# Cross attention of a decoder: scores seven pairs ahead, keys three batches ahead, queries stacked for two batches

## The chip, the cores and the metric

One core of a Trainium2 chip runs the whole kernel in one launch. The metric is the device time of that launch in microseconds. Three runs of the kernel before took 4714.99, 4725.56 and 4725.31 us; their median is 4725.31.

## The reference

A decoder of four layers works on x, 32 batches of 56 tokens of 128 features, all in float32. Layers 1, 2 and 3 each have a cross attention to the same context of 1500 rows for each batch, and that is the part that the change touches:

```python
Q = (query @ Wq + bq).reshape(B, Sq, H, D).transpose(0, 2, 1, 3)   # query = layernorm(x): 32 x 56 x 128
K = (key @ Wk + bk).reshape(B, Sk, H, D).transpose(0, 2, 1, 3)     # key = value = ctx: 32 x 1500 x 128
V = (value @ Wv + bv).reshape(B, Sk, H, D).transpose(0, 2, 1, 3)
scores = jnp.einsum('bhqd,bhkd->bhqk', Q, K) / jnp.sqrt(jnp.float32(D))   # H = 16 heads, D = 8
attn = jax.nn.softmax(scores, axis=-1)
out = jnp.einsum('bhqk,bhkd->bhqd', attn, V).transpose(0, 2, 1, 3).reshape(B, Sq, E)
x = x + (out @ Wo + bo)
```

Layer 2 divides by the root of 128 instead. The other parts (self attention, a recurrence, mixtures of experts, a linear and a rotary attention) stay as they are.

## The kernel before

`decoder` (L2597) runs one stage after the other; `cross_attention` (L893) is called for layers 1, 2 and 3. Each engine has its own program in it, with the order of its work written out by hand, and semaphores between the engines.

The sixteen heads are eight pairs. A score product keeps float32 precision with bfloat16 matmuls: keys and queries are each split into three bfloat16 parts (high, middle, low), and six products of parts are wanted. So 96 rows are stacked, six slots (`SLOTS`) of 16 features, by DMAs on SP's queue (L984 for keys, L989 for queries): six DMAs for each half (four pairs) of a batch. Source buffers (`key_parts`) and stacked buffers (`keys`, `queries`) are double, the context `ctx_t` is threefold, and three banks hold one pair's scores.

The main loop has a pass i for each batch, and a pass has eight steps, one for each pair. In step p of pass i TensorE (L1122) does, in this order:

- `scores_by_key(i, p)` (L1063, matmuls L1072): twelve matmuls that give the scores with keys on the partitions, less the row maximum, which sits as additional rows of the stacked queries. It waits for the exponential of the pair before, since the three TURNED banks are single;
- in steps 3 and 7 `turn_tops` (L1058, L1061), which transposes the row maxima of four pairs; it waits for GpSimd's `split_tops` (L1230, operations L1234 to L1238);
- in steps 1 to 3 a third of the keys of batch i + 2, `make_keys` (L1026, L1034); in step 4 `fold` (L1089, L1098) of batch i - 1; in steps 5 to 7 a third of the values of batch i + 1, `make_values` (L1036, L1045). All of these share one bank, TURNS;
- `scores` (L1048, L1055) for the pair LEAD = 6 steps ahead: three matmuls of 500 keys, each of which waits until VectorE has taken the maximum of the pair before out of its bank;
- in steps 0 and 4 `mix_values` (L1076, L1085): 96 matmuls of probabilities by values for four pairs.

ScalarE (L1207) has `exponentials` (L1182, L1184) in each step, `place_others` (L1178, L1180) ahead of it in steps 0 and 4, `keep_mixed` (L1187) in steps 1 and 5, and behind the exponential the copy of a third of the keys (`keep_keys` L1165, L1171) or values (`keep_values` L1173, L1175) out of TURNS. VectorE (L1368) has `place_first` (L1339, L1341) in steps 3 and 7, the three row maxima of a pair in each step (`row_tops` L1323, L1326), `join_tops` (L1328) behind the last pair of a half, `keep_mix` (L1343) in step 4, and behind that `last_parts` (L1311, L1315 to L1321), which splits the last third of the keys of batch i + 2. GpSimd (L1261) splits the other two thirds (`high_part` L1247, L1250 and L1252; `low_parts` L1254, L1257 and L1259) and does `split_tops` between them. SP (L1010) loads context i + 3, then stacks both halves of batch i + 2 (`stack`, L973).

Ahead of the loop a head makes the normalisation, the queries and the keys of batch 0 (`lead_keys` L1021, `lead_high_part` L1289, `lead_low_parts` L1240, L1243), and the loop starts at pass -1, in which only the parts that run ahead have work.

## Time and profile before

| | |
|---|---|
| median of three runs | 4725.31 us |
| the profiled execution: its own time | 4729.11 us |
| the profiled execution: its span | 4727.3 us |
| mean granted TensorE clock | 0.921 of full |
| instructions | 107462 |

The span is that of the one profiled execution, from its first to its last record; its own time is measured around it and is 1.8 us longer. Engine names in rows: PE is TensorE's matmuls and PEld its weight loads, DVE is VectorE, ACT is ScalarE, POOL is GpSimd, SPq is SP's DMA queue. A timeline row is start, busy time, engine, line of the kernel, output and input, count, and in brackets the idle time of the engine ahead of it with what ended it. A row with a count merges neighbours; ends of matmuls are modelled and can overlap the next start.

### The profile page before, as it was taken

Reading aid. Unit: us, or ns where it says so; the run is one execution under the profiler, and the core shown is the slowest. Engines: PE = TensorE matmul, PEld = TensorE weight load, DVE = VectorE, ACT = ScalarE, POOL = GpSimd, SP = SyncE. Lnnn points to the kernel's source line nnn. Section 1 sums busy time; section 2 is a strip of 40 time slices with the busy share of each in tenths; the row PEclk is TensorE's granted clock in tenths of the full one; section 3 lists DMA queues with packets and bytes.
Section 4 is the critical chain, followed back from the end, with each engine's and each line's share of the span. In section 5 each row is a group of like instructions: output and inputs, shape, how many; then the busy total and the mean of one; then the engine's idle time right before and its main releaser. Section 6 shows DMA issues by size and latency. Waiting matters only on the chain. (4 is left out here: it accounts for less than half of the span.)

```text
span 4727.3 us, 107462 instructions
## 1 busy us (share of the span) xinstructions
PE 3885.6 (82%) x44766; PEld 2680.4 (57%) x44766; DVE 2978.1 (63%) x4986; ACT 2181.7 (46%) x2885; POOL 1144.9 (24%) x1441
## 2 busy tenths in 40 slices
PE   7987559999996977799999979866779999995498
PEld 5864226666664446466666654333346666663376
DVE  5632468877774445488777743355668787773643
ACT  2234436656663233266666643433346666663010
POOL 0000024444440000144444410021434444430000
PEclk9989869999997999899999989978789999996689
DMA  3035035555551410355555511000045555550366
GB/s 131 0 117 201 2 88 134 139 133 137 136 135 33 115 45 0 68 140 134 139 138 138 135 44 63 24 4 4 0 108 141 134 140 137 137 129 1 81 178 159
DMA packets 251804, 463.48 MB, mean 98 GB/s; under 512 B 135598, under 2 KB 143278, under 8 KB 251086
## 3 DMA queue, kind: packets, MB, share of 16 engines
q1 hardware_dynamic: 251406, 457.76, 38.1%
q8 instruction: 301, 4.93, 0.4%
q14 instruction: 97, 0.79, 0.0%
HBM read 212.85 MB, written 1.72 MB: 45 GB/s over the span
## 5 line engine op out<-in xcount | busy, mean ns | idle before, releaser
L1326 DVE TENSOR_REDUCE x_bank_top<-ps 112x1 f32<-112x500 f32 x2304 | 1409.7, 670 | 457.9 <-PE ps L1055 446.2
L1184 ACT ACTIVATE x_probs_t<-ps 128x1344 f32<-128x1344 f32 x768 | 990.9, 1290 | 309.1 <-PE ps L1072 296.3
L1055 PE MATMUL ps<-x_keys,x_queries 96*112 96x500 bf16 x2304 | 697.2, 387 | 62.8 <-DVE x_bank_top L1326 34.7
L1072 PEld LDWEIGHTS ps<-x_queries,x_keys 128*128 128x128 bf16 x9216 | 504.1, 98 | 189.6 <-ACT x_probs_t L1184 90.6
L1072 PE MATMUL ps<-x_queries,x_keys 128*128 128x112 bf16 x9216 | 585.8, 213 | 30.9 <-ACT x_probs_t L1184 25.0
L1055 PEld LDWEIGHTS ps<-x_keys,x_queries 96*112 96x112 bf16 x2304 | 288.7, 131 | 391.9 <-DVE x_bank_top L1326 198.2
L1085 PE MATMUL ps<-x_probs_t,x_values 128*32 128x112 f32 x18432 | 491.2, 263 | 4.1 <-ACT x_probs_t L1184 4.1
L1085 PEld LDWEIGHTS ps<-x_probs_t,x_values 128*32 128x32 f32 x18432 | 444.4, 111 | 51.0 <-issue 43.0
L1250 POOL TENSOR_TENSOR x_key_part<-x_key_whole,x_nothing 128x500 bf16<-128x500 f32 x186 | 231.3, 1244 | 826.0 <-ACT x_key_whole L1171 826.0
L1034 PE MATMUL ps<-x_ctx_t,x_wk 128*128 128x500 f32 x558 | 311.3, 640 | 25.5 <-ACT x_key_whole L1171 15.5
L1045 PE MATMUL ps<-x_wv,x_ctx_t 128*128 128x128 f32 (+1 forms) x2304 | 328.8, 286 | 1.7 <-issue 1.6
L1274 POOL MEMSET x_nothing<- 128x500 f32 x3 | 1.5, 514 | 1180.6 <-issue 1180.6
L1045 PEld LDWEIGHTS ps<-x_wv,x_ctx_t 128*128 128x128 f32 (+1 forms) x2304 | 280.3, 191 | 8.4 <-issue 1.8
L1189 ACT COPY x_mixed<-ps 128x112 f32<-128x112 f32 x192 | 48.4, 252 | 480.3 <-PE ps L1085 480.3
L1171 ACT ACTIVATE x_key_whole<-ps,x_bk 128x500 f32<-128x500 f32 x279 | 188.3, 675 | 127.0 <-PE ps L1034 103.6
L1257 POOL TENSOR_TENSOR x_key_part<-x_key_left,x_nothing 128x500 bf16<-128x500 f32 x186 | 233.7, 1256 | 7.5
L1517 PE MATMUL ps<-xn_lead,e_w 128*128 128x448 f32 x512 | 224.9, 546 | 4.2 <-DMA e_share<-m_weight_rows 4.2
L1259 POOL TENSOR_TENSOR x_key_part<-x_key_left,x_key_part 128x500 bf16<-128x500 f32 x186 | 218.0, 1172 | 14.6
L1544 ACT ACTIVATE e_silu<-ps 128x448 f32<-128x448 f32 x192 | 104.3, 543 | 249.5 <-PE ps L1517 249.5
L1252 POOL TENSOR_TENSOR x_key_left<-x_key_whole,x_key_part 128x500 f32<-128x500 f32 x186 | 211.6, 1138 | 14.6
L1523 PE MATMUL ps<-e_hidden,e_w 128*128 128x448 f32 x384 | 181.5, 554 | 9.1 <-DVE e_hidden L1562 5.0
L1175 ACT COPY x_values<-ps 128x512 f32<-128x512 f32 x288 | 168.2, 584 | 38.6 <-PE ps L1045 28.7
(478 smaller groups left out, 5340.2 us busy)
## 6 DMA issues: line engine op xcount, KB each, us to landing
x_keys<-x_key_part SPq DMA_DIRECT2D x1152, 192.0 KB, 3.5
x_ctx_t<-in_ctx_t SPq DMA_DIRECT2D x96, 750.0 KB, 4.6
cm_ctx_n<-in_ctx_n SPq DMA_DIRECT2D x32, 768.0 KB, 6.0
cm_ctx_t<-in_ctx_t SPq DMA_DIRECT2D x32, 750.0 KB, 8.3
x_queries<-x_query_part SPq DMA_DIRECT2D x1152, 14.0 KB, 2.3
e_share<-m_weight_scratch SPq DMA_DIRECT2D x32, 490.0 KB
e_spread_out<-m_slot_scratch SPq DMA_DIRECT2D x32, 490.0 KB
e_share<-m_weight_rows SPq DMA_DIRECT2D x32, 448.0 KB, 5.8
```

The costliest lines, as they stand in the source:

```text
L1034: nc.tensor.matmul(ps[:, TURNS, 0:KB], wk[:], ctx_t[i % CONTEXTS][:, KB * n:KB * n + KB], start=True, stop=True).then_inc(k_done, 1)
L1045: mm = nc.tensor.matmul(ps[0:ROWS[k], TURNS, P * c:P * c + P], ctx_t[i % CONTEXTS][:, CHUNK[k]], wv[:], start=True, stop=True)
L1055: nc.tensor.matmul(ps[0:RW, n, 0:KB], queries[i % 2][0:TALL, p, :], keys[i % 2][0:TALL, p, KB * n:KB * n + KB], start=True, stop=True).the ...
L1072: mm = nc.tensor.matmul(ps[:, TURNED + c // VC, RW * (c % VC):RW * (c % VC) + RW], keys[i % 2][:, p, KT * c:KT * c + KT], queries[i % 2][: ...
L1085: mm = nc.tensor.matmul(ps[32 * g:32 * g + 32, MIX, RW * h:RW * h + RW], values[i % 2][0:ROWS[c], c, (PF + 1) * p:(PF + 1) * p + 32], prob ...
L1184: nc.scalar.activation(probs_t[PROBS[p]].rearrange("k (n c) r -> k n (c r)", c=VC), ps[:, TURNED:TURNED + VR, 0:VC * RW], ACT.Exp, scale=s ...
L1250: nc.gpsimd.tensor_tensor(part[0][:, cols], key_whole[n][:], nothing[:], ALU.add).then_inc(k_high, 1)
L1252: nc.gpsimd.tensor_tensor(key_left[0][:], key_whole[n][:], part[0][:, cols], ALU.subtract).then_inc(k_rest, 1)
L1257: nc.gpsimd.tensor_tensor(part[1][:, cols], key_left[0][:], nothing[:], ALU.add).then_inc(k_mid, 1)
L1259: nc.gpsimd.tensor_tensor(part[2][:, cols], key_left[0][:], part[1][:, cols], ALU.subtract).then_inc(k_low, 1)
L1326: nc.vector.tensor_reduce(bank_top[0:RW, p, n:n + 1], ps[0:RW, n, 0:KB], AX_X, ALU.max).then_inc(topped, 1)
L1517: mm = nc.tensor.matmul(ps[:, 4 + 2 * (n % 2) + m, 0:CT], w[u][:, s, m, :], tokens[c], start=True, stop=True)
```

## The change

- **Lead.** LEAD goes from 6 to 7, so scores run seven pairs ahead; `turn_tops` and `place_first` move from steps 3 and 7 to steps 2 and 6.
- **Keys.** `make_keys` and `keep_keys` work on batch i + 3 instead of i + 2 and move from steps 1 to 3 to steps 5 to 7, on TensorE behind the step's scores; values move from steps 5 to 7 to steps 1 to 3. The loop starts at pass -2.
- **High parts.** For the second and last third ScalarE writes the bfloat16 high part straight from the bank, with an activation of its own ahead of the copy. GpSimd makes the high part of the first third and the middle and low parts of all three (`key_third`); `last_parts` on VectorE is gone. GpSimd's order in a pass is the split of the first half of batch i + 1, two thirds, the split of the second half, the last third.
- **Stacking.** Keys and queries have semaphores of their own. Queries are stacked for two batches at once, so six query DMAs of twice the bytes serve a half of two batches; ScalarE's queue issues the first six. SP's pass has the two halves of the keys with queries and the context between them, and contexts are loaded four batches ahead.
- **Head.** GpSimd fills the value buffers with ones ahead of `lead_low_parts`, not behind it.
- Waits follow: `make_keys` and `make_values` wait for `mix_kept` and `added` of other batches, `fold` and `project` for the work that now comes before them on the shared bank.

The core of the diff (buffers' indices that follow from the new shape of `queries`, removed functions and declarations are left out):

```diff
-LEAD = 6
+LEAD = 7
...
-    KEY_STEPS, VALUE_STEPS, FOLD_STEP = (1, 2, 3), (5, 6, 7), 4
-    BY_POOL = NB_ - 1
    TURNED, MIX, TURNS = 3, 6, 7
+    VALUE_STEPS, FOLD_STEP, KEY_STEPS = (1, 2, 3), 4, (5, 6, 7)
...
-        queries = [sbuf("queries%d" % u, [P, PR, RW], BF16) for u in range(2)]
+        queries = [sbuf("queries%d" % u, [P, PR, 2, RW], BF16) for u in range(2)]
...
+        def query_slots(engine, e, h, s):
+            source = slice(64 * h, 64 * h + 64)
+            queries_of = query_parts[QUERY_PART[s]][source]
+            engine.dma_start(queries[e % 2][s:TALL:SLOTS, HP_ * h:HP_ * h + HP_].rearrange("r p b n -> r (p b n)"),
+                             queries_of[:, 2 * e:2 * e + 2].rearrange("f b c s -> f (b c s)")).then_inc(queries_stacked[e % 2][h], 16)
...
@@ sync @@
+            def stack_keys(i, h):
+                u = i % 2
+                wait(sp, turned_done, PR * (i - 2) + HP_ * (h + 1))
+                if i == 0:
+                    sp.wait_ge(lead_low, NB_)
+                else:
+                    sp.wait_ge(k_low, NB_ * i)
+                source = slice(64 * h, 64 * h + 64)
+                for s in range(SLOTS):
+                    sp.dma_start(keys[u][s:TALL:SLOTS, HP_ * h:HP_ * h + HP_].rearrange("r p n -> r (p n)"),
+                                 key_parts[u][KEY_PART[s]][source]).then_inc(keys_stacked[u][h], 16)
+            def stack_queries(e, h):
+                wait(sp, turned_done, PR * (2 * e - 3) + HP_ * (h + 1))
+                sp.wait_ge(q_low, 2 * (2 * e // CB) + 2)
+                for s in range(SLOTS):
+                    query_slots(sp, e, h, s)
...
+            context(2)
             sp.wait_ge(zeros_ready, 2 * PARTS)
-            for h in range(2):
-                stack(0, h)
+            stack_keys(0, 0)
+            stack_keys(0, 1)
+            stack_queries(0, 1)
+            stack_keys(1, 0)
+            stack_keys(1, 1)
+            context(3)
             def one_pass(i):
-                if has(i + 3):
-                    context(i + 3)
+                if i % 2 == 1 and has(i + 1):
+                    stack_queries((i + 1) // 2, 1)
                 if has(i + 2):
-                    for h in range(2):
-                        stack(i + 2, h)
-            for i in range(-1, B):
+                    stack_keys(i + 2, 0)
+                if has(i + CONTEXTS + 1):
+                    context(i + CONTEXTS + 1)
+                if i % 2 == 0 and has(i + 2):
+                    stack_queries(i // 2 + 1, 0)
+                if has(i + 2):
+                    stack_keys(i + 2, 1)
+            for i in range(B):
                 one_pass(i)
@@ tensor @@
                     wait(pe, v_kept, VR * (i - 1))
-                    wait(pe, added, min((i - 3) // CB, CH - 1))
+                    wait(pe, mix_kept, i - 3)
...
-                    if step == 3 and has(i):
+                    if step == 2 and has(i):
                         turn_tops(i, 1)
-                    if step == 7 and has(i + 1):
+                    if step == 6 and has(i + 1):
                         turn_tops(i + 1, 0)
-                    if step in KEY_STEPS and has(i + 2):
-                        make_keys(i + 2, KEY_STEPS.index(step))
+                    if step in VALUE_STEPS and has(i + 1):
+                        make_values(i + 1, VALUE_STEPS.index(step))
                     if step == FOLD_STEP and has(i - 1):
                         fold(i - 1)
-                    if step in VALUE_STEPS and has(i + 1):
-                        make_values(i + 1, VALUE_STEPS.index(step))
                     ahead, pair = divmod(step + LEAD, PR)
                     if has(i + ahead):
                         scores(i + ahead, pair)
+                    if step in KEY_STEPS and has(i + 3):
+                        make_keys(i + 3, KEY_STEPS.index(step))
                     if step == 0 and has(i - 1):
                         mix_values(i - 1, 1)
                     if step == HP_ and has(i):
                         mix_values(i, 0)
-            for i in range(-1, B + 1):
+            for i in range(-2, B + 1):
@@ scalar @@
                 act.wait_ge(k_done, NB_ * (i - 1) + n + 1)
-                if n < BY_POOL:
-                    wait(act, k_low, BY_POOL * (i - 2) + n + 1)
-                else:
-                    wait(act, last_low, i - 1)
+                if n > 0:
+                    wait(act, keys_stacked[i % 2][1], SLOTS * 16 * (i // 2))
+                    nc.scalar.activation(key_parts[i % 2][0][:, KB * n:KB * n + KB], ps[:, TURNS, 0:KB], ACT.Identity, bias=bk[:, 0:1])
+                if i == 1:
+                    act.wait_ge(lead_low, n + 1)
+                wait(act, k_low, NB_ * (i - 2) + n + 1)
                 nc.scalar.activation(key_whole[n][:], ps[:, TURNS, 0:KB], ACT.Identity, bias=bk[:, 0:1]).then_inc(k_kept, 1)
...
             mid_query(0)
+            act.wait_ge(q_low, 2)
+            for s in range(SLOTS):
+                query_slots(act, 0, 0, s)
@@ gpsimd @@
+            def key_third(i, n):
+                part, cols, before = key_parts[i % 2], slice(KB * n, KB * n + KB), NB_ * (i - 1) + n
+                pool.wait_ge(k_kept, before + 1)
+                if n == 0:
+                    wait(pool, keys_stacked[i % 2][1], SLOTS * 16 * (i // 2))
+                    nc.gpsimd.tensor_tensor(part[0][:, cols], key_whole[n][:], nothing[:], ALU.add).then_inc(k_high, 1)
+                    pool.wait_ge(k_high, i)
+                else:
+                    pool.wait_ge(k_low, before)
+                nc.gpsimd.tensor_tensor(key_left[:], key_whole[n][:], part[0][:, cols], ALU.subtract).then_inc(k_rest, 1)
+                pool.wait_ge(k_rest, before + 1)
+                nc.gpsimd.tensor_tensor(part[1][:, cols], key_left[:], nothing[:], ALU.add).then_inc(k_mid, 1)
+                pool.wait_ge(k_mid, before + 1)
+                nc.gpsimd.tensor_tensor(part[2][:, cols], key_left[:], part[1][:, cols], ALU.subtract).then_inc(k_low, 1)
             def one_pass(i):
-                if has(i + 2):
-                    high_part(i + 2, 0)
-                if has(i):
-                    split_tops(i, 1)
-                if has(i + 2):
-                    low_parts(i + 2, 0)
-                    high_part(i + 2, 1)
-                    low_parts(i + 2, 1)
                 if has(i + 1):
                     split_tops(i + 1, 0)
+                if has(i + 3):
+                    key_third(i + 3, 0)
+                    key_third(i + 3, 1)
+                if has(i + 1):
+                    split_tops(i + 1, 1)
+                if has(i + 3):
+                    key_third(i + 3, 2)
@@ vector @@
-                    if step == 3 and has(i):
+                    if step == 2 and has(i):
                         place_first(i, 1)
-                    if step == 7 and has(i + 1):
+                    if step == 6 and has(i + 1):
                         place_first(i + 1, 0)
...
-                    if step == FOLD_STEP and has(i + 2):
-                        last_parts(i + 2)
```

## Rows read from the trace of the kernel before

**Rows 1.** The page, part 1: busy time, share of the span, instructions

```profile
PE 3885.6 (82%) x44766; PEld 2680.4 (57%) x44766; DVE 2978.1 (63%) x4986; ACT 2181.7 (46%) x2885; POOL 1144.9 (24%) x1441
```

**Rows 2.** Windows 1000:1240, columns PE, PEld, DVE, ACT, POOL, then PEclk, DMA, GB/s

```profile
1000.00:1240.00 240.00, 226.07 (x3569) 165.89 (x3568) 189.96 (x358) 149.30 (x177) 102.73 (x135) 1.00 0.56 134
```

**Rows 3.** Timeline of TensorE, one pass: start us, busy us, engine, line

```profile
1003.18 0.77 PE L1072 MATMUL ps<-x_queries,x_keys 128*128 128x112 bf16 x12
...
1003.78 1.12 PE L1045 MATMUL ps<-x_wv,x_ctx_t 128*128 128x128 f32 x8
...
1004.74 0.80 PE L1055 MATMUL ps<-x_keys,x_queries 96*112 96x500 bf16 x3
...
1005.38 0.75 PE L1072 MATMUL ps<-x_queries,x_keys 128*128 128x112 bf16 x12
...
1008.10 0.76 PE L1072 MATMUL ps<-x_queries,x_keys 128*128 128x112 bf16 x12
...
1010.73 0.75 PE L1072 MATMUL ps<-x_queries,x_keys 128*128 128x112 bf16 x12
...
1015.20 0.77 PE L1072 MATMUL ps<-x_queries,x_keys 128*128 128x112 bf16 x12
...
1017.35 0.77 PE L1072 MATMUL ps<-x_queries,x_keys 128*128 128x112 bf16 x12
...
1019.63 0.75 PE L1072 MATMUL ps<-x_queries,x_keys 128*128 128x112 bf16 x12
...
1021.29 0.22 PE L1061 MATMUL ps<-x_ident_low,x_top_parts 128*32 128x112 bf16 x1 [0.91 <-POOL x_top_parts L1238]
...
1023.02 0.75 PE L1072 MATMUL ps<-x_queries,x_keys 128*128 128x112 bf16 x12
...
1023.71 0.68 PE L1098 MATMUL ps<-x_mixed,x_place 128*64 128x56 f32 x16
...
1024.32 0.84 PE L1055 MATMUL ps<-x_keys,x_queries 96*112 96x500 bf16 x3
...
1025.09 2.51 PE L1085 MATMUL ps<-x_probs_t,x_values 128*32 128x112 f32 x96
...
1027.53 0.76 PE L1072 MATMUL ps<-x_queries,x_keys 128*128 128x112 bf16 x12
```

**Rows 4.** Timeline of the other engines and SP's queue in that pass

```profile
1003.36 1.50 DVE L1317 TENSOR_TENSOR x_key_left<-x_key_whole,x_key_part 128x500 f32<-128x500 f32 x1
...
1005.95 1.84 DVE L1326 TENSOR_REDUCE x_bank_top<-ps 112x1 f32<-112x500 f32 x3
...
1006.11 4.29 SPq L984 DMA_DIRECT2D x_keys<-x_key_part  x6
...
1016.00 1.29 ACT L1184 ACTIVATE x_probs_t<-ps 128x1344 f32<-128x1344 f32 x1 [0.41 <-PE ps L1072]
...
1020.48 0.20 POOL L1234 TENSOR_TENSOR x_top_left<-x_top,x_top_parts 112x4 f32<-112x4 f32 x1
```

**Rows 5.** Groups of instructions, window 1000:1240: GpSimd's first key part, ScalarE's key copy

```profile
L1250 POOL TENSOR_TENSOR x_key_part<-x_key_whole,x_nothing 128x500 bf16<-128x500 f32 x20 | 24.9, 1245 | 91.8 <-ACT x_key_whole L1171 91.8
...
L1171 ACT ACTIVATE x_key_whole<-ps,x_bk 128x500 f32<-128x500 f32 x29 | 19.6, 675 | 8.2 <-PE ps L1034 7.9
```

**Rows 6.** Timeline, the head of the first cross attention

```profile
658.38 1.61 POOL L1243 TENSOR_TENSOR x_key_part<-x_key_whole,x_nothing 128x500 bf16<-128x500 f32 x1 [1.23 <-DVE x_key_whole L1295]
...
668.91 2.04 PE L1034 MATMUL ps<-x_ctx_t,x_wk 128*128 128x500 f32 x2 [4.86 <-ACT x_key_whole L1171]
...
675.10 1.50 PE L1055 MATMUL ps<-x_keys,x_queries 96*112 96x500 bf16 x3 [4.15 <-DMA x_queries<-x_query_part]
...
689.23 0.76 PE L1072 MATMUL ps<-x_queries,x_keys 128*128 128x112 bf16 x12
```

**Rows 7.** Timeline of TensorE, passes 30 and 31: the second mix of a batch

```profile
1429.20 2.51 PE L1085 MATMUL ps<-x_probs_t,x_values 128*32 128x112 f32 x96
...
1451.54 2.51 PE L1085 MATMUL ps<-x_probs_t,x_values 128*32 128x112 f32 x96
```

70 lines of the change are left out of this document (21 added, 49 removed).

## The prediction

> **What bounds the kernel now.** I read the page first: TensorE is the busiest engine over the span, VectorE next [rows 1]. Then a steady stretch of a cross attention, 1000 to 1240 us: TensorE is busy 226.07 of 240 us at full clock, VectorE 189.96, ScalarE 149.30, GpSimd 102.73 [rows 2]. So TensorE's queue is the thing to time. Its busy time overlaps (three score matmuls are busy 0.80, the next work starts 0.64 after them), so I use starts. The timeline shows one pass, from one step 5 (1003.18) to the next (1027.53): 24.35 us. The first starts of scores_by_key mark the steps [rows 3]: step 5 takes 2.20, 6 takes 2.72, 7 takes 2.63, 0 takes 4.47, 1 takes 2.15, 2 takes 2.28, 3 takes 3.39, 4 takes 4.51. The pieces come from the same starts: scores_by_key holds the queue for 0.60 (0.69 ahead of fold), values 0.96, scores 0.64, fold 0.61, a mix 2.44. Step 1, with a key matmul, is 2.15, which leaves about 0.90 for that.
>
> The pieces alone give 2.15 to 2.20 for a step with keys or values. The excess sits in two places. Step 3: the turn of the tops waits 0.91 for GpSimd [rows 3], which begins the three-part split only at 1020.48, behind key work [rows 4]. Steps 6, 7 and 0 hold about 1.5 in all: VectorE works off last_parts (its subtraction alone 1003.36 to 1004.86) and starts the maxima of step 5, 1.84 for three, at 1005.95 [rows 4], although their scores had begun at 1004.74; each later pair of scores finds its banks late.
> A second loop is close behind: an exponential, 1.29, starts when scores_by_key has ended (0.41 idle before it) [rows 4], and the next scores_by_key waits for it: 0.77 + 1.29 and two handovers are the 2.15 of step 1.
>
> **The change, part by part**, in the steady pass, with scores_by_key of step 5 starting at time 0.
>
> *All three key thirds to GpSimd.* VectorE is busy 19.3 of 24.35 now [rows 2] and loses four operations, about 3 us (from before 1003.36 to the maxima at 1005.95). It keeps 16.3, and scores come at least 2.15 apart while maxima take 1.84. The waits for banks in steps 6, 7 and 0 should go.
>
> *LEAD 7, turns at steps 2 and 6.* From a half's last scores to its turn it is two steps, as before, but now with a mix of 2.44 in them. The split takes 0.81 (1020.48 to 1021.29).
>
> *Two high parts a pass by ScalarE.* Each is priced as its key copy, 0.675 [rows 5]; it could be 0.58 if neighbours overlap by 0.1. In step 5 the key matmul, now behind the scores, ends at 2.34; copy to 3.06. scores_by_key(6) starts 2.14, exp(6) runs 3.09 to 4.38. Turn (0.15), scores and key matmul of step 6 end 4.63; two activations to 6.0, so exp(7), whose scores are ready at 5.2, runs 6.03 to 7.32, and scores_by_key(0) starts at 7.37: here the new work costs 0.8. The two activations of step 7 and place_others end 9.2, exp(0) 10.5, under the mix, which ends 11.2. Steps 1 to 3, now with values: 2.20, 2.40 with the turn, 2.20. Step 4: 0.69 + 0.61 + 0.64 + 2.44, taken as 4.35. Pass: 2.14 + 2.28 + 2.95 + 3.83 + 2.20 + 2.40 + 2.20 + 4.35 = 22.35, **2.0 less**.
>
> *GpSimd* gets four operations for third 0 and three for each other, at 1.24 as its first one [rows 5]: 3.1 to 8.1, then to 11.9. The tops of the second half are ready at 10.5, their split queues behind third 1 and ends 12.75; the turn at 14.0 is not held. Third 2 ends at 16.5. In all some 14 of 22.35.
>
> *SP* issues 12 key, on average 6 query and 1 context DMA a pass instead of 25; six take 4.29 [rows 4]. The first half of stack_keys waits for the turned scores of step 3 (16.6), is issued by 21 and landed by 25; it is needed in step 1 of the next pass, 33.5. The second: turned 27.5, landed 35.5, in odd passes queries behind it 39; needed 45. I cost stacking, contexts and the longer query rows at nothing: this slack of 6 to 10 hides them, and each us beyond would be a us of the pass. ScalarE's new wait for the stacked keys, with exponentials queued behind it, and GpSimd's, want a landing at 13 (the pass before's second half) and stand at 24.5 and 25: no cost.
>
> *Ends of a stage.* Passes 0 to 28 gain 2.0 each: 58. Two mixes a pass apart without keys are 22.34 apart now [rows 7]; by the pieces such a pass needs 21.3, and after the change there are two, one of them full before: 3.0 + 1.0 = 4. In the head the first scores start at 675.10, on the queries' DMA, and the first scores_by_key at 689.23 [rows 6]. After, two more key matmuls at 2.04 each [rows 6], each followed by ScalarE, and the first values stand ahead of the first scores: those start near 677.8. Three pairs with values, slow at first, end 685.5, pairs four and five 688.2 (VectorE's 1.84 each), then the split before the turn 689.5, pairs six and seven with keys 692.9: scores_by_key at 693.5. I take +4, with -3 and +9 as bounds.
> The six query DMAs that ScalarE gets in the head lie in this: no row shows it issuing one. By SP's rows six hold it for 4.3 [rows 4], with the first key copy behind them. Between about 0 (handing over alone) and 8.6 (the queues alternate) I take 4.3, the same shape on SP.
> By the Trainium skill ("DMA: Bandwidth & Descriptors", Issuing engines are not separate DMA queues) both queues share the DMA engines, and a second one saves only sequencer time. By that the 8.6 holds, and the sum is 13 us higher.
>
> **Sum:** -58 - 4 + 4 = -58 for a stage, and the same function runs three times: -174. The profiled execution took 4729.1 (span 4727.3), so 4555. The median of the runs, 4725.3, lies 3.8 lower: **4551**.
>
> **Rivals.**
> *TensorE is full.* It is busy 94.2% [rows 2], so only 5.8% of 24.35, 1.4 us, can go: 29 x 1.4 x 3 = 122, 4603. If ScalarE's 0.4 comes on top, the pass gains 1.0: 29 x 1.0 x 3 = 87, 4638. Against it stands 0.80 busy for 0.64 of queue [rows 3]; for it, only that 94.2% leaves little to find.
> The Trainium skill ("Trainium Kernel Development and Optimization", Performance Expectations) calls matmul busy time a bad metric, since matmuls are pipelined; by that rule this rival falls, and the 0.80 against 0.64 agrees.
> *The second activation hides.* Then step 7 nears 2.2 and the pass 21.35: 3 x 29 x 3 = 261 less, 4464. Against: the next key matmul waits for the bank that both activations read.
> *GpSimd stretches: slower.* In the head one key operation took 1.61 beside VectorE's two-operand work [rows 6]. Place: the split of the second half, behind thirds 0 and 1. Those seven operations have 10.1 us before the turn waits, 1.44 each; at 1.73 the gain of a pass is gone, and from there it is slower. At 2.2 the turn comes 5.3 late, the pass is 27.6: 29 x 3.3 x 3 = 287 more, 5012. For: every split has a third ahead of it. Against: the partner of the 1.61 is what the change takes off VectorE in the pass; its maxima take one operand, from PSUM.
> *Nothing happens:* another loop sets 24.35. Against: the step times above are the sum of named pieces and waits. 4725.
>
> **Chances.** Forecast (pass 1.7 to 2.4 shorter) 0.50; TensorE full, in either form, 0.28; hidden activation 0.13; nothing 0.03; slower 0.06. The forecast's own range is 4516 to 4578, with the head's bounds 4495 to 4593. The whole range takes in the second case, to 4640, and reaches towards the third, 4485. About 0.3% (14 us) can be told from no change. Faster 0.91, same 0.03, slower 0.06.
>
> **What would show it.** Right: eight steps in 22.2 to 22.6; no turn waiting for GpSimd; step 7 near 2.9, with two activations ahead of its exponential; VectorE busy near 16.3 of 22.4; the first scores_by_key some 4 us later in its stage. Wrong: scores that wait for a stacking DMA or still for maxima; a split that ends after scores_by_key(2); GpSimd operations above 1.44; step 7 at 2.2.

## The result and the profile after

The changed kernel takes 4574.1 us (median of four runs, 4572.3 to 4578.1), against 4723.4 for four runs of the kernel before on the same chip: a ratio of 0.9688, with an interval of 0.9672 to 0.9705. Forecast were 4551 (4485 to 4640) and a faster kernel. So the sign and the size hold; of the 174 us that the sum took off, about 150 came. The profiled span is 4572.2, against 4727.3 before.

The page, part 1, after:

```profile
PE 3829.8 (84%) x44766; PEld 2651.2 (58%) x44766; DVE 2742.5 (60%) x4614; ACT 2282.7 (50%) x3071; POOL 1363.5 (30%) x1627
```

Against [rows 1] VectorE lost 372 instructions, which is four for each of 31 batches and three stages; ScalarE gained 186, and GpSimd 186. The window 1000:1240, which answers to [rows 2] (columns PE, PEld, DVE, ACT, POOL, then PEclk, DMA, GB/s):

```profile
1000.00:1240.00 240.00, 234.90 (x3814) 173.52 (x3802) 174.34 (x341) 172.16 (x212) 137.91 (x170) 1.00 0.61 149
```

TensorE is at 97.9% of busy time now, and VectorE is busy 16.3 us of a pass (174.34 of 240), as the prediction had it. The steady pass is 22.43 us in the median of a stage, from mix to mix (11.04 with steps 5 to 0, 11.39 with steps 1 to 4), against 24.35 (12.02 and 12.33) before. Timeline of TensorE, answering to [rows 3]; the first row stands at step 6:

```profile
1004.65 0.76 PE L1091 MATMUL ps<-x_queries,x_keys 128*128 128x112 bf16 x12
1005.34 0.22 PE L1080 MATMUL ps<-x_ident_low,x_top_parts 128*32 128x112 bf16 x1
...
1007.01 0.75 PE L1091 MATMUL ps<-x_queries,x_keys 128*128 128x112 bf16 x12
...
1009.78 0.75 PE L1091 MATMUL ps<-x_queries,x_keys 128*128 128x112 bf16 x12 [0.17 <-ACT x_probs_t L1204]
...
1013.54 0.77 PE L1091 MATMUL ps<-x_queries,x_keys 128*128 128x112 bf16 x12
...
1015.73 0.75 PE L1091 MATMUL ps<-x_queries,x_keys 128*128 128x112 bf16 x12
1016.41 0.22 PE L1080 MATMUL ps<-x_ident_low,x_top_parts 128*32 128x112 bf16 x1
...
1018.20 0.75 PE L1091 MATMUL ps<-x_queries,x_keys 128*128 128x112 bf16 x12
...
1020.43 0.75 PE L1091 MATMUL ps<-x_queries,x_keys 128*128 128x112 bf16 x12
...
1024.93 0.76 PE L1091 MATMUL ps<-x_queries,x_keys 128*128 128x112 bf16 x12
...
1027.07 0.77 PE L1091 MATMUL ps<-x_queries,x_keys 128*128 128x112 bf16 x12
```

By the starts step 6 takes 2.36, 7 takes 2.77, 0 takes 3.76, 1 takes 2.19, 2 takes 2.47, 3 takes 2.23, 4 takes 4.50 and 5 takes 2.14. Neither turn waits. Step 7 is held by ScalarE, as the other engines' timeline shows:

```profile
1005.95 1.85 DVE L1338 TENSOR_REDUCE x_bank_top<-ps 112x1 f32<-112x500 f32 x3
...
1007.21 0.68 ACT L1187 ACTIVATE x_key_part<-ps,x_bk 128x500 bf16<-128x500 f32 x1 [0.48 <-PE ps L1050]
...
1007.79 0.67 ACT L1191 ACTIVATE x_key_whole<-ps,x_bk 128x500 f32<-128x500 f32 x1
...
1008.35 1.29 ACT L1204 ACTIVATE x_probs_t<-ps 128x1344 f32<-128x1344 f32 x1
...
1014.38 0.20 POOL L1257 TENSOR_TENSOR x_top_left<-x_top,x_top_parts 112x4 f32<-112x4 f32 x1
```

The two activations of step 6 run from 1007.21 to 1008.35, and the exponential of step 7, whose scores began at 1007.01, waits for them. VectorE's maxima now start right behind their scores. GpSimd's split, behind two thirds, starts at 1014.38 and is done 1.3 before the turn. Groups in the same window, answering to [rows 5] (busy us, mean ns of one, idle before):

```profile
L1187 ACT ACTIVATE x_key_part<-ps,x_bk 128x500 bf16<-128x500 f32 x22 | 14.9, 677 | 5.4 <-PE ps L1050 5.2
L1276 POOL TENSOR_TENSOR x_key_part<-x_key_whole,x_nothing 128x500 bf16<-128x500 f32 x11 | 13.7, 1244 | 32.9 <-ACT x_key_whole L1191 32.9
L1280 POOL TENSOR_TENSOR x_key_left<-x_key_whole,x_key_part 128x500 f32<-128x500 f32 x32 | 36.3, 1135 | 2.4
```

In this window no GpSimd operation is stretched. In the first six passes of a stage two are, where VectorE still splits queries: the last operation of the second key third takes 1.40 instead of 1.14, and the first of the tops' split behind it 0.58 instead of 0.20. This is absorbed, as no turn waits there either. The head of the first cross attention, answering to [rows 6]:

```profile
663.38 5.00 ACTq L961 DMA_DIRECT2D x_queries<-x_query_part  x6
...
668.57 0.68 ACT L1191 ACTIVATE x_key_whole<-ps,x_bk 128x500 f32<-128x500 f32 x1 [8.15 <-issue]
...
677.97 1.46 PE L1074 MATMUL ps<-x_keys,x_queries 96*112 96x500 bf16 x3
...
692.41 0.75 PE L1091 MATMUL ps<-x_queries,x_keys 128*128 128x112 bf16 x12
```

Between the first matmul of the head's keys and the first scores_by_key there are 41.2 us (from 651.25), against 37.3 before (from 651.91): 3.8 more. In the second and third head it is 41.3 and 41.2 against 38.9 and 37.0. The second stage, from the start of its first mix to that of its last, took 763.3 before; after:

```profile
1960.26 2.51 PE L1104 MATMUL ps<-x_probs_t,x_values 128*32 128x112 f32 x96
...
2668.90 3.40 PE L1104 MATMUL ps<-x_probs_t,x_values 128*32 128x112 f32 x68 [1.38 <-ACT x_probs_t L1204]
```

That is 708.6. The three stages together went from 2298.4 to 2130.8, by 167.6; the three heads gave back 3.8, 2.4 and 4.2, together 10.5. The difference, 157.1, is what the span lost (155.1) but for 2 us.

### The profile page after: what moved, and what is told of

It is laid out like the page before. It is cut to its first block and busy times, and to the rows that moved or that the text cites. A ratio compares the mean times of both kernels' runs of the same rounds, so it can differ in the third digit from the quotient of the medians.

```text
span 4572.2 us, 107234 instructions
## 1 busy us (share of the span) xinstructions
PE 3829.8 (84%) x44766; PEld 2651.2 (58%) x44766; DVE 2742.5 (60%) x4614; ACT 2282.7 (50%) x3071; POOL 1363.5 (30%) x1627
## 5 line engine op out<-in xcount | busy, mean ns | idle before, releaser
L1091 PEld LDWEIGHTS ps<-x_queries,x_keys 128*128 128x128 bf16 x9216 | 487.5, 98 | 348.9 <-issue 167.6
L1074 PE MATMUL ps<-x_keys,x_queries 96*112 96x500 bf16 x2304 | 632.1, 380 | 5.1 <-DVE x_bank_top L1338 3.9
L1282 POOL TENSOR_TENSOR x_key_part<-x_key_left,x_nothing 128x500 bf16<-128x500 f32 x279 | 347.6, 1246 | 21.9
L1050 PE MATMUL ps<-x_ctx_t,x_wk 128*128 128x500 f32 x558 | 298.1, 616 | 41.8 <-ACT x_key_whole L1191 21.6
L1284 POOL TENSOR_TENSOR x_key_part<-x_key_left,x_key_part 128x500 bf16<-128x500 f32 x279 | 321.3, 1152 | 21.9
L1280 POOL TENSOR_TENSOR x_key_left<-x_key_whole,x_key_part 128x500 f32<-128x500 f32 x279 | 316.8, 1135 | 21.1
L1074 PEld LDWEIGHTS ps<-x_keys,x_queries 96*112 96x112 bf16 x2304 | 258.9, 131 | 107.3 <-DVE x_bank_top L1338 33.2
L1257 POOL TENSOR_TENSOR x_top_left<-x_top,x_top_parts 112x4 f32<-112x4 f32 x192 | 45.4, 236 | 616.2 <-DVE x_top L1349 615.2
L1276 POOL TENSOR_TENSOR x_key_part<-x_key_whole,x_nothing 128x500 bf16<-128x500 f32 x93 | 115.6, 1243 | 269.0 <-ACT x_key_whole L1191 269.0
```

Of the source, the lines that this page charges most:

```text
L1050: nc.tensor.matmul(ps[:, TURNS, 0:KB], wk[:], ctx_t[i % CONTEXTS][:, KB * n:KB * n + KB], start=True, stop=True).then_inc(k_done, 1)
L1074: nc.tensor.matmul(ps[0:RW, n, 0:KB], queries[i // 2 % 2][0:TALL, p, i % 2, :], keys[i % 2][0:TALL, p, KB * n:KB * n + KB], start=True, st ...
L1091: mm = nc.tensor.matmul(ps[:, TURNED + c // VC, RW * (c % VC):RW * (c % VC) + RW], keys[i % 2][:, p, KT * c:KT * c + KT], queries[i // 2 % ...
L1280: nc.gpsimd.tensor_tensor(key_left[:], key_whole[n][:], part[0][:, cols], ALU.subtract).then_inc(k_rest, 1)
L1282: nc.gpsimd.tensor_tensor(part[1][:, cols], key_left[:], nothing[:], ALU.add).then_inc(k_mid, 1)
L1284: nc.gpsimd.tensor_tensor(part[2][:, cols], key_left[:], part[1][:, cols], ALU.subtract).then_inc(k_low, 1)
```

## The experiments

Each kernel is one edit of the kernel before or of the changed one. "Half" is the time from one mix to the next: one half holds steps 5 to 0, the other steps 1 to 4. Kernels differ by more than their edits: the parts outside the three stages and their heads, which no edit touches, took 2268 to 2283 us in the fourteen profiled executions, and stalls of TensorE (last section) add up to 14 us in the stages. A difference of less than some 15 us between two kernels is therefore read here from the steady passes, not from the times. Experiments 4, 5 and 6 are one run each.

### 1. Before, GpSimd splits the tops ahead of the first key part

```diff
-                if has(i + 2):
-                    high_part(i + 2, 0)
                 if has(i):
                     split_tops(i, 1)
                 if has(i + 2):
+                    high_part(i + 2, 0)
                     low_parts(i + 2, 0)
```

> The kernel before, with GpSimd's split of the second half's tops ahead of the first key third and not between its operations; nothing else. Theory (the schedule of the prediction): the turn in step 3 no longer waits 0.91 us, the pass goes from 24.35 to about 23.45, 30 passes in three stages give -81: 4643, with the waits for banks unchanged. Rival (TensorE is full, its starts cannot come closer): 4725 and the 0.9 turns up as another wait.

Measured: 4832.2 us, ratio 1.0224 (1.0199 to 1.0250). The half with steps 1 to 4 did fall from 12.33 to 11.35, as the turn no longer waits. But the other rose from 12.02 to 13.7 in about half of the passes and to between 14.5 and 15.1 in most of the others. GpSimd's key work starts later and now lies beside VectorE's last_parts. Timeline of one pass, and groups in 1000:1240, of that kernel:

```profile
1009.40 1.56 POOL L1257 TENSOR_TENSOR x_key_part<-x_key_left,x_nothing 128x500 bf16<-128x500 f32 x1
...
1009.89 1.35 DVE L1318 CAST x_key_part<-x_key_left 128x500 bf16<-128x500 f32 x1
```

```profile
L1316 DVE TENSOR_TENSOR x_key_left<-x_key_whole,x_key_part 128x500 f32<-128x500 f32 x9 | 13.4, 1494 | 0.3
L1320 DVE TENSOR_TENSOR x_key_part<-x_key_left,x_key_part 128x500 bf16<-128x500 f32 x9 | 12.7, 1408 | 0.3
L1318 DVE CAST x_key_part<-x_key_left 128x500 bf16<-128x500 f32 x9 | 11.2, 1245 | 0.3
```

In the kernel before these three take 1416, 679 and 421 ns. With the fourth, the cast of the high part (565 before, 526 here), 3.1 us became 4.7. The maxima wait behind them, and TensorE for the banks:

```profile
1013.50 0.91 PE L1055 MATMUL ps<-x_keys,x_queries 96*112 96x500 bf16 x2 [1.36 <-DVE x_bank_top L1325]
...
1015.00 1.33 PE L1072 MATMUL ps<-x_queries,x_keys 128*128 128x112 bf16 x12
```

The second row shows a second loss: behind this wait of 1.36 the granted clock falls to its lower level (0.50 from 1015.0 to 1018.0), and the twelve matmuls are busy 1.33 instead of 0.76. In the second stage passes at full clock take 25.06, and those in which it fell, about half, 26.0 to 26.4 at a mean clock of 0.93. So the waits for banks make 1.7 us of the longer half, and the clock another 1.0 to 1.3 where it falls.

So the turn's wait in the kernel before could not be had back by an exchange of two calls: the order with the wait kept GpSimd's and VectorE's key work further apart. By the Trainium skill ("SBUF — State Buffer", Who interferes with whom) a VectorE instruction with two SBUF inputs contends with a GpSimd instruction that reads SBUF, and a cast can contend when it runs in a 2-port mode. The rows agree for the subtractions (679 against 1408 ns) and for one of the casts (421 against 1245); in which mode the casts ran no row shows.

### 2. Before, GpSimd splits the last third as well

```diff
-    BY_POOL = NB_ - 1
+    BY_POOL = NB_
...
                     low_parts(i + 2, 1)
+                    high_part(i + 2, 2)
+                    low_parts(i + 2, 2)
                 if has(i + 1):
                     split_tops(i + 1, 0)
...
-                    if step == FOLD_STEP and has(i + 2):
-                        last_parts(i + 2)
```

> The kernel before, with last_parts taken off VectorE: GpSimd does the last third as it does the others, still two batches ahead. Theory: the waits for banks go (-1.5 a pass), but the third ends some 3 us later, so the split of the next first half queues behind it (about +1.2) and stacking ends after the scores want it (+1.4 or more): pass 24.0 to 26, time 4690 to 4880, with scores that wait for a stacking DMA in the trace. Rival (the move off VectorE is the gain by itself, keys three ahead are not needed): pass 22.9, 4595.

Measured: 4830.4 us, ratio 1.0224 (1.0188 to 1.0261), inside the theory's range, but by other terms than it names. The turn in step 7 waits, in nearly every pass:

```profile
1020.50 0.22 PE L1060 MATMUL ps<-x_ident_low,x_top_parts 128*32 128x112 bf16 x1 [1.69 <-POOL x_top_parts L1234]
```

The turn in step 3 waits 0.92, as before. Scores hardly wait for a stacking DMA, which the theory expected: 2.1 us in the three stages together, though in many passes the queries land with nothing to spare. And of the waits for banks only those of step 6 go (2.18 instead of 2.72); step 0 stays at 4.47. The half with steps 5 to 0 goes from 12.02 to 13.07, and to some 14 in the passes in which the granted clock falls (25.40 for a pass at full clock, 26.3 to 26.5 for one at a mean of 0.94).

### 3. Before, all thirds by GpSimd in the order of the change

The edit of 2, and in GpSimd's pass:

```diff
+                if has(i):
+                    split_tops(i, 1)
                 if has(i + 2):
                     high_part(i + 2, 0)
-                if has(i):
-                    split_tops(i, 1)
-                if has(i + 2):
                     low_parts(i + 2, 0)
                     high_part(i + 2, 1)
                     low_parts(i + 2, 1)
-                    high_part(i + 2, 2)
-                    low_parts(i + 2, 2)
                 if has(i + 1):
                     split_tops(i + 1, 0)
+                if has(i + 2):
+                    high_part(i + 2, 2)
+                    low_parts(i + 2, 2)
```

> The kernel before with GpSimd's part of the change alone: all three thirds of the keys split by GpSimd (last_parts on VectorE removed), in the change's order (split of one half, two thirds, split of the other half, last third), but keys still made two batches ahead in steps 1 to 3, LEAD 6, and SP's queue as before. Theory (the keys three batches ahead are what makes room for that order): in the rows of before the tops of the second half are split by about 1019.4, two thirds last to 1029, the split of the next half waits for its tops to about 1031.3, and the last third ends near 1036.9. Then SP issues six key and six query DMAs, 8.6, landed 1.4 later, 1046.9, for the scores in step 2 of the next pass, which stand 2.9 behind the start of its step 1 (1015.20 plus a pass): the pass is at least 28.8. That is 4.45 x 29 x 3 = 387 more: 5000 to 5150, with a wait of the scores for the stacked queries in step 2 of every pass. Rival (VectorE's relief and the order carry the gain by themselves, and the transfers are hidden): the halves are 10.5 and 11.4, the pass 21.9, 4500 to 4530.

Measured: 5311.3 us, ratio 1.1234 (1.1153 to 1.1314). The mechanism is the one named, and the loss is larger than its range: the pass is 30.6. Timelines of SP and of TensorE in that kernel, and its window:

```profile
1028.67 4.52 SPq L983 DMA_DIRECT2D x_keys<-x_key_part  x6
1033.23 4.36 SPq L988 DMA_DIRECT2D x_queries<-x_query_part  x6
```

```profile
1038.81 1.50 PE L1054 MATMUL ps<-x_keys,x_queries 96*112 96x500 bf16 x3 [4.83 <-DMA x_queries<-x_query_part]
1040.10 1.33 PE L1071 MATMUL ps<-x_queries,x_keys 128*128 128x112 bf16 x12
...
1041.56 2.04 PE L1033 MATMUL ps<-x_ctx_t,x_wk 128*128 128x500 f32 x2
...
1056.85 0.92 PE L1054 MATMUL ps<-x_keys,x_queries 96*112 96x500 bf16 x2
1057.94 0.42 PE L1054 MATMUL ps<-x_keys,x_queries 96*112 96x500 bf16 x1 [0.17 <-DVE x_bank_top L1312]
```

```profile
1000.00:1240.00 240.00, 198.13 (x2762) 140.58 (x2760) 128.01 (x251) 118.24 (x141) 118.56 (x141) 0.89 0.46 111
```

SP, which waits for the last third, starts at 1028.67, the twelve DMAs are issued by 1037.6, and the scores start 1.2 later, 4.8 late. What I had not priced is the clock: behind that wait TensorE is granted the lower of its two levels (1.2 instead of 2.4 GHz), three score matmuls are busy 1.50 instead of 0.80 and two key matmuls 2.04 instead of the 1.11 of step 2, until about 1045.2, 6.4 us behind the start of these scores. The half with steps 1 to 4 is 19.3 instead of the 11.35 of experiment 1; less a wait of about 4.9 that leaves 3 for the clock. In the change, where keys are three batches ahead, the same order leaves no scores waiting for a stacking DMA. No run moves the keys alone. But experiments 6, 8 and 10 have them ahead without one each of the other aids (high parts by ScalarE, LEAD 7, queries by two) and keep passes of 22.1 to 22.5 in the median. So it is by elimination that the batch ahead makes the room.

The last two rows are the scores of step 0. VectorE has no key work in this kernel, and yet the third matmul waits for a bank, and step 0 takes 4.47 as before (step 6 falls from 2.72 to 2.18, step 7 from 2.64 to 2.46). The scores of step 0 start 1.23 behind those of step 7 in both kernels (1055.62 and 1056.85 here, 1010.09 and 1011.32 before), and VectorE needs 1.84 for one pair. So last_parts made some 0.7 of the 1.5 us of waits for banks, and the close scores of steps 7 and 0 the other 0.7.

### 4. Changed kernel, the split behind all three thirds

```diff
                     key_third(i + 3, 1)
-                if has(i + 1):
-                    split_tops(i + 1, 1)
-                if has(i + 3):
                     key_third(i + 3, 2)
+                if has(i + 1):
+                    split_tops(i + 1, 1)
```

> The changed kernel, with GpSimd's split of the second half behind all three thirds instead of behind two. Theory: the last third ends 15.6 after step 5, the split 16.4, the turn at 14.0 waits 2.4 a pass: pass 24.8, 29 x 2.4 x 3 = 209 more than 4574: 4783. Rival (the turn has slack that the trace does not show, or another wait is only exchanged): within 30 of 4574.

Measured: 4907.5 us, 124 above the theory. The wait is as expected:

```profile
1022.41 0.22 PE L1080 MATMUL ps<-x_ident_low,x_top_parts 128*32 128x112 bf16 x1 [2.45 <-POOL x_top_parts L1261]
```

```profile
1000.00:1240.00 240.00, 215.69 (x3383) 160.99 (x3383) 153.81 (x300) 150.42 (x185) 117.15 (x147) 0.96 0.53 130
```

Some passes take the expected 24.94, at full clock, but most 26.5, at a mean clock of 0.94: behind the idle stretch the granted clock falls to its lower level (0.96 over the window, 1.00 in the changed kernel), and 1.6 more go. The split between the thirds is needed, and a late turn costs more than its wait.

### 5. Changed kernel with VectorE's removed load put back as idle work

Four operations of the kinds of last_parts, on data of their own, behind keep_mix in step 4; they compute nothing that is used.

```diff
                         keep_mix(i - 1)
+                        extra_parts(i - 1)
```

> The changed kernel, with four operations of last_parts' shapes on spare buffers given back to VectorE in step 4, for which nobody waits. Theory: they start the maxima of step 5 some 2.3 late and the scores of steps 6 to 0 wait for banks, 1.5 a pass as before the change, less what ScalarE's hold of step 7 covers: pass 23.1 to 23.9, time 4635 to 4705. Rival (the bank waits went because scores now come ahead of the key matmuls and a pair earlier, not because of VectorE's load): pass 22.4 to 22.7, 4574 to 4600.

Measured: 4648.8 us. The pass is 23.19, and the whole of the 0.76 lies in step 6 (3.13 instead of 2.37), where scores wait for banks. Step 0 stays at 3.76: with the load on VectorE again its wait does not come back. So VectorE's relief is worth about 75 us of the gain, by what is late when it is undone. The load is lighter than the one taken off: beside no work of GpSimd the four operations take 410, 680, 421 and 679 ns, 2.2 us, against 3.1 in the kernel before.

### 6. Changed kernel, GpSimd makes all high parts

```diff
@@ scalar @@
-                if n > 0:
-                    wait(act, keys_stacked[i % 2][1], SLOTS * 16 * (i // 2))
-                    nc.scalar.activation(key_parts[i % 2][0][:, KB * n:KB * n + KB], ps[:, TURNS, 0:KB], ACT.Identity, bias=bk[:, 0:1])
@@ gpsimd @@
                 if n == 0:
                     wait(pool, keys_stacked[i % 2][1], SLOTS * 16 * (i // 2))
-                    nc.gpsimd.tensor_tensor(part[0][:, cols], key_whole[n][:], nothing[:], ALU.add).then_inc(k_high, 1)
-                    pool.wait_ge(k_high, i)
                 else:
                     pool.wait_ge(k_low, before)
+                nc.gpsimd.tensor_tensor(part[0][:, cols], key_whole[n][:], nothing[:], ALU.add).then_inc(k_high, 1)
+                pool.wait_ge(k_high, before + 1)
```

> The changed kernel, with all high parts by GpSimd, none by ScalarE. Theory: step 7 gains its 0.55 as well, but the second third ends 1.25 later and the split behind it makes the turn of step 2 wait about 0.6: pass 22.3 to 22.6, 4565 to 4590. Rival (the split has slack to spare): pass 21.9, 4526. Rival (GpSimd's operations stretch): above 4600.

Measured: 4569.4 us, the pass 22.47. The half with steps 5 to 0 falls to 10.49, as ScalarE has nothing ahead of the exponential of step 7; the other rises to 11.97, as step 2 is 0.58 longer and the turn in it waits 0.50 for GpSimd (1.03 in the first six passes of a stage). Two effects of half a us cancel.

### 7. Changed kernel, VectorE makes the second high part

The high part of the middle third is a cast on VectorE in step 7, from the float32 copy; ScalarE keeps that of the last third.

```diff
+            def second_high_part(i):
+                wait(dve, keys_stacked[i % 2][1], SLOTS * 16 * (i // 2))
+                dve.wait_ge(k_kept, NB_ * (i - 1) + 2)
+                nc.vector.tensor_copy(key_parts[i % 2][0][:, KB:2 * KB], key_whole[1][:]).then_inc(second_high, 1)
```

> The changed kernel, with the high part of the second key third made by VectorE (one cast behind the maxima of step 7) instead of by ScalarE; ScalarE keeps the one of the last third. Theory: the first of ScalarE's two activations in step 6 is what holds the exponential of step 7; without it step 7 falls from 2.77 to about 2.2, while the one of the last third stays hidden by the mix. Pass 21.85 to 21.9, 29 x 0.55 x 3 = 48 less: 4526. Rival (TensorE or another loop sets step 7, or VectorE's cast brings waits for banks back): pass 22.3 or more, 4565 to 4600.

Measured: 4537.4 us, ratio 0.9609 (0.9591 to 0.9626). Step 7 takes 2.22, the half with steps 5 to 0 is 10.49, the pass 21.88. The cast costs VectorE this:

```profile
1008.38 0.41 DVE L1342 CAST x_key_part<-x_key_whole 128x500 bf16<-128x500 f32 x1
```

It costs GpSimd more: its operation beside the cast takes 1.80 instead of 1.14, so the tops' split ends later. In the first six passes of a stage VectorE splits queries as well, and two more GpSimd operations take 1.51 and 1.40 instead of 1.25 and 1.14. There the turn in step 2 waits 0.40 for the split (18 waits, 7.0 us in all), and the half with steps 1 to 4 is 0.47 longer; this is most of what lies between 4537 and the 4526 expected.

### 8. Changed kernel with LEAD 6, turns in steps 3 and 7

```diff
-LEAD = 7
+LEAD = 6
...
-                    if step == 2 and has(i):
+                    if step == 3 and has(i):
                         turn_tops(i, 1)
-                    if step == 6 and has(i + 1):
+                    if step == 7 and has(i + 1):
                         turn_tops(i + 1, 0)
```

(and place_first with them)

> The changed kernel with LEAD 6 and the turns and first placements in steps 3 and 7 again; all else as changed. Theory: the seventh pair is worth next to nothing by itself, since the tops of a half are ready some 0.5 before the turn that follows two steps later: pass 22.4 to 22.7, 4565 to 4595. Rival (the distance was what removed the waits): the turn waits again 0.5 to 1, pass 23 to 23.5, 4625 to 4670.

Measured: 4547.3 us, ratio 0.9629 (0.9605 to 0.9653): faster than the change, and both expectations fell. Steps 5 to 0 of that kernel:

```profile
1022.86 0.76 PE L1091 MATMUL ps<-x_queries,x_keys 128*128 128x112 bf16 x12
...
1025.00 0.76 PE L1091 MATMUL ps<-x_queries,x_keys 128*128 128x112 bf16 x12
...
1027.15 0.76 PE L1091 MATMUL ps<-x_queries,x_keys 128*128 128x112 bf16 x12
...
1029.85 0.75 PE L1091 MATMUL ps<-x_queries,x_keys 128*128 128x112 bf16 x12 [0.17 <-ACT x_probs_t L1204]
...
1033.61 0.76 PE L1091 MATMUL ps<-x_queries,x_keys 128*128 128x112 bf16 x12
```

Step 6 takes 2.15 instead of 2.36, step 7 takes 2.70 instead of 2.77. Step 7 waits for an exponential anyway, so the turn costs nothing there; in step 6 it stands ahead of the scores, the key matmul and all that ScalarE does next.

### 9. Changed kernel, LEAD 7 kept, turns in steps 3 and 7

The edit of 8 without its first line.

> The changed kernel with LEAD 7 kept, and turns and place_first moved back to steps 3 and 7. It tells apart what the run with LEAD 6 did. Theory (the step of the turn matters, the seventh pair ahead does not): the turn's 0.23 leaves step 6, where it stands ahead of the scores and the key matmul and so ahead of the copies and the exponential of step 7; pass near 22.1, as with LEAD 6, 4545 to 4555. Rival (the seventh pair ahead is what costs): pass stays near 22.43, 4570 to 4580.

Measured: the steady pass is 22.10 with the same four step times as in experiment 8, so the theory holds: the step of the turn decides, and the seventh pair ahead neither costs nor gives anything in the pass. The time is 4567.0 (4560.6 to 4575.5), not 4545 to 4555, and not told apart from the change. The profiled execution is 26.3 us longer than that of experiment 8. Of this 14.9 lie in the stages, though their steady passes are equal: the halves exceed their medians by 37.5 us in all, against 23.5 in experiment 8 and 19.4 in the changed kernel. In each of the three, 13.5 of this are the nine passes with a projection; most of the rest are stalls at which no record shows a releaser. What makes them is open. Another 13.0 lie in parts that the edit does not touch. Against the changed kernel the late turns also cost 7.0 in the three heads (168.0 to the first mix, against 161.0). So the 0.33 of the pass is shown, and a shorter time for it with LEAD 7 is not.

### 10. Changed kernel, queries stacked for one batch at a time

```diff
+            for b in range(2):
+                engine.dma_start(queries[e % 2][s:TALL:SLOTS, HP_ * h:HP_ * h + HP_, b],
+                                 queries_of[:, 2 * e + b]).then_inc(queries_stacked[e % 2][h], 16)
```

> The changed kernel, with each query DMA issued as two, one for each batch: 25 DMAs a pass on SP's queue again instead of 19 on average. Theory: landings have 6 us and more to spare in the steady pass, only the head can move by some us: 4570 to 4590. Rival (SP's queue was the bound that stacking by two removed): pass above 22.8 with scores waiting for DMAs, 4610 and more.

Measured: 4631.6 us, ratio 0.9807 (0.9782 to 0.9833), the rival's time. The median pass stays 22.43, but every second to fourth is 1 to 2 us longer, a few more. SP's queue and the scores of step 5 (pair four) in the second pass:

```profile
715.74 8.49 SPq L962 DMA_DIRECT2D x_queries<-x_query_part  x12
724.34 5.37 SPq L989 DMA_DIRECT2D x_keys<-x_key_part  x6
729.75 9.94 SPq L962 DMA_DIRECT2D x_queries<-x_query_part  x12
```

```profile
740.95 1.41 PE L1075 MATMUL ps<-x_keys,x_queries 96*112 96x500 bf16 x3 [2.00 <-issue]
```

A DMA of half the bytes holds SP as long as a whole one, 0.71 against 0.72 to 0.79 us. Twelve take 8.5 to 9.9; the last of the second twelve is issued at 739.7, and the scores that need them start at 740.95. The trace names no releaser for this wait, but seventeen such waits of scores stand in the three stages, 19.6 us in all, against none in the changed kernel, and fifteen of them end 1.2 to 3.1 us after SP has issued twelve query DMAs. In the head ScalarE issues twelve, in 10.8 us, and the first scores come some 6 later. Of the 53 us between the two profiled executions 31 lie in the stages and 20 in the three heads. So stacking by two is worth 57 us in this arrangement, the difference of the medians: it is no extra, it is what keeps the transfers hidden.

### 11. Changed kernel, SP issues the first six query DMAs

```diff
-            act.wait_ge(q_low, 2)
-            for s in range(SLOTS):
-                query_slots(act, 0, 0, s)
...
             stack_keys(0, 0)
+            stack_queries(0, 0)
             stack_keys(0, 1)
```

> The changed kernel with the first six query DMAs issued by SP, between the two halves of the stacked keys, instead of by ScalarE. In the changed kernel these six held ScalarE for 5.00 us in the head (663.38 to 668.38) with the first key copy behind them. Theory (ScalarE's queue is what the head waits for): the first scores start some 2 to 3 us earlier than 677.97, near 675, and the first scores_by_key near 690; 3 x 2.5 less, about 4566. Rival (the sharing of SP's queue costs as much as it saves: six DMAs are 4.3 of SP, so the second half of the keys lands later): scores_by_key stays at 692 or later, 4574 to 4590. The steady pass stays 22.43 in both.

Measured: 4568.0 us (two runs), ratio 0.9662 (0.9642 to 0.9682), not told apart from the change. Counted from the first matmul of the head's keys (654.08 in this run), the first scores come after 23.3 instead of 26.7, 3.4 sooner, but the first scores_by_key after 41.2, as in the change. There the granted clock is back at its lower level from 687 to 693, and a pair of key matmuls is busy 1.87; in the change it is full in this stretch, and they take 1.00. In the second and third head the first scores_by_key come after 38.0 and 39.8, against 41.3 and 41.2. So ScalarE's issue held the first scores, and in two heads of three the end as well; the 4.7 us of that are too few to show in the time.

### 12. The two gains together: LEAD 6, late turns, second high part by VectorE

The edits of 7 and 8.

> The changed kernel with LEAD 6 and turns and place_first in steps 3 and 7 (as in the run with LEAD 6 alone, 22.10 a pass) and the high part of the second third made by VectorE in step 7 (as in the run with that alone, which shortened the half with steps 5 to 0 by 0.55). Theory (the two gains are of different steps and add): step 7 falls from 2.70 to about 2.2, the pass to 21.55; 0.55 x 29 x 3 = 48 less than the 4547 of LEAD 6 alone, of which the first passes of a stage may take 7 back: 4500 to 4510. Rival (both took away the same hold of the exponential of step 7, so only the larger one is left): pass 21.9, 4530 to 4540. A second rival: the split of the first half on GpSimd or VectorE's later start holds the turn in step 7, seen as a wait of the turn for L1261: pass above 22, 4550 or more.

Measured: 4531.7 us (five runs, 4516.3 to 4537.3), ratio 0.9579 (0.9559 to 0.9600): the lowest median of all, though its interval meets that of experiment 7. Starts of steps 7, 0 and 1:

```profile
1022.78 0.76 PE L1092 MATMUL ps<-x_queries,x_keys 128*128 128x112 bf16 x12
...
1025.15 0.75 PE L1092 MATMUL ps<-x_queries,x_keys 128*128 128x112 bf16 x12
...
1028.91 0.76 PE L1092 MATMUL ps<-x_queries,x_keys 128*128 128x112 bf16 x12
```

The pass is 21.76: the gains of 0.55 and 0.33 share 0.21 of step 7 (2.37 here, 2.22 in experiment 7), since the turn now stands in the step that has been freed. The time falls between theory and rival, and that it is lower than experiment 7's is not shown. A projection pass costs 1.83 more than a normal one here; the projection behind the scores of step 0, instead of ahead of them, was not tried.

## Why the prediction was right, point by point

- **VectorE's relief ends the waits for banks.** Right that they end; right for about half of them that VectorE's relief does it. Experiment 5 gives back 0.76 a pass by a load alone, all in step 6. The 0.71 that step 0 lost (4.47 to 3.76) has another cause: experiments 2 and 3 relieve VectorE and keep 4.47, experiment 5 loads it and keeps 3.76. In the change the key matmul stands behind the scores of step 7, and the scores of step 0 start 2.77 behind them (1007.60 and 1010.37 in the pass shown), not 1.23, so VectorE's 1.84 fits in between. The prediction's "scores come at least 2.15 apart" covers this, but it books the whole under VectorE. No run moves the key matmul alone, so this is argued; but experiments 4 to 10 undo one by one the other parts of the change, save the batch ahead and the steps of keys and values, and all keep step 0 at 3.76.
- **The parts don't pay by themselves.** The prediction does not say this. Neither the order on GpSimd nor the move to GpSimd nor both pay in the kernel before: the first runs into VectorE's last_parts and the clock, the second into both turns, the third into the stacking and the clock.
- **LEAD 7 with turns a step earlier.** The prediction gives it no gain, and it brings none: experiment 9 leaves the pass alone with LEAD 7, and the early turns cost 0.33 of it (experiments 8 and 9).
- **The turn no longer waits.** Right; the split is done 1.3 ahead of it, and experiment 4 brings the wait back at 2.45, at the place of the third rival (the order made the delay, not a stretched GpSimd).
- **Two activations hold step 7.** Right in place: taking one away gives 0.55 (experiment 7), and taking both no more (2.22 in experiment 6 too), so the rival in which they hide falls. The size was taken too large, 2.95 against 2.77: the new work costs 0.55, not 0.8.
- **Steps.** Forecast 22.35, measured 22.43. Step 7 was 0.18 too long in the sum and step 0 0.07; steps 2, 4 and 6 were 0.07, 0.15 and 0.08 too short. The 0.08 that is left is 7 us over 29 passes and three stages.
- **TensorE is full.** This rival had 0.28 and is refuted: the busy share rose from 94.2% to 97.9% while the pass lost 1.9 us, and in experiment 12 it is 98.2% with 0.67 us less still. Starts of matmuls in its queue, not busy shares, gave the floor.
- **GpSimd stretches.** Not where it counts: 1244 and 1135 ns in the steady passes, and what is stretched in the first six is absorbed. The price of its contention is real all the same, as experiment 1 shows from VectorE's side and experiment 7 from GpSimd's.
- **Transfers hidden.** Right, but with less room than "6 to 10" says: experiment 10 spends it with twelve more issues in two passes.
- **The head.** +3.8, +2.4 and +4.2, 3.5 on average, for the +4 of the sum. The first scores come at 677.97 for 677.8, but that is in part luck: this head began 0.66 earlier than before, so they are 0.8 late. The six DMAs on ScalarE took 5.00, for 4.3, and not the 8.6 that the prediction held possible.
- **What was mis-sized.** Two terms of the ends. The projection, which I had not looked at, stands ahead of the scores in step 0 and uses the shared bank; with keys in step 7 it now waits for ScalarE's copy:

```profile
895.63 0.99 PE L1123 MATMUL ps<-x_mix,x_wo 128*128 128x448 f32 x2 [0.51 <-ACT x_key_whole L1191]
```

A pass with it is 1.50 longer than a normal one, against 0.66 before: 0.84 for nine of them is 7.6. And the last passes of a stage gave 2.4, not 4: they take 21.69 and 21.49, not 21.3, and the first of the two was 23.05 before, not full. That is 4.8 over the stages. With the 7 of the steps the sum is 19, as much as the profiled executions differ from the forecast (155 against 174). That it closes so well is partly chance: stalls and untouched parts move a time by as much.

## What to carry to other kernels

Take work off an engine only with a look at where the receiving engine's other duties fall due: the same move was part of a gain of 150 us with the split between the thirds and the keys a batch earlier, and cost 100 to 590 us without them. Look at the starts of two successive consumers of the same banks, too: in step 0 a wait went because the producer's work was spread, not because the engine that empties the banks had less to do. A small operation in an in-order queue belongs in the step that waits anyway, not one step sooner. And where a change can leave TensorE idle for some us in each pass, price the clock as well as the wait.

## What was not expected of the hardware

- After waits of TensorE of 1.36 us (experiment 1), 2.45 us (experiment 4) and 4.83 us (experiment 3) the granted clock fell to its lower level, and matmuls behind them took up to twice as long: 1.0 to 1.3 us more in half of the passes of experiment 1, 1.6 in most of experiment 4, about 3 in those of experiment 3. Not every such wait does it: the same 2.45 is followed by full clock in other passes of experiment 4, and the clock is 1.00 over the window shown of the kernel before, with its 0.91 in every pass. In a profile of the changed kernel the same stretch stands at full clock.
- Four VectorE operations on SBUF data took 4.7 us where they lay beside GpSimd's for most of their time (experiment 1), 3.1 in the kernel before and 2.2 beside none (experiment 5); a bfloat16 cast went from 421 to 1245 ns, and GpSimd's own operation in that place from 1.25 to 1.56.
- A stacking DMA's time on SP does not depend on its bytes here: 0.71 for one batch of queries, 0.72 to 0.79 for two.
- TensorE stalls of 0.8 us and more with no releaser stand in the stages of every kernel but that of experiment 3, as between the eleventh and the twelfth matmul of a scores_by_key in the changed kernel:

```profile
1003.04 0.22 PE L1091 MATMUL ps<-x_queries,x_keys 128*128 128x112 bf16 x1 [1.58 <-issue]
```

They sum to 3.6 us over the three stages of the changed kernel (three stalls) and to 14.4 in experiment 9 (nine), lie elsewhere in each kernel, and bound what a comparison of two kernels can tell.
